# In a slot, the weight copy ahead of plan pieces and results, and plan pieces at other steps

## The reference, cut to what matters

```python
# x [32, 128, 128], ctx [32, 128, 256], mask [32, 128]; 8 heads of 16; 8 experts of 512; fp32
h = layernorm(x)
kv = (ctx @ W_src.T + b_src) * mask;  q = (h @ W_tgt.T + b_tgt) * mask
attn = softmax(where(mask == 0, -inf, q @ k.T / 4));  upd = attn @ v
x = x + tanh(g_xattn) * (concat([h, upd]) @ W_out.T + b_out)
t = layernorm(x)
p = softmax(t @ router_w.T);  top 2 of 8, weights renormalised
x = x + tanh(g_ffn) * sum over the 2 experts e of weight * (gelu(t @ w1[e]) @ w2[e])
```

## Time and profile before

| | us |
|---|---|
| median of 3 runs (lowest, highest) | 334.58 (333.62, 334.91) |
| the profiled execution, its span | 335.18, 333.4 |
| PE busy | 301.5 (90%) |
| weight loads (PEld) | 267.2 (80%) |
| DVE busy | 213.8 (64%) |
| POOL busy | 202.9 (61%) |
| ACT busy | 189.2 (57%) |
| mean granted TensorE clock | 0.974 |

### The profile page before, as it was taken

How to read it: one execution, slowest core, us unless ns; L and a number is a source line. 1 busy time by engine, 2 the same in 40 slices (tenths; PEclk the granted TensorE clock), 3 DMA queues, 4 the chain that set the end, 5 groups by cost and what they waited for, 6 DMA issues and landing times.

```text
span 333.4 us, 11014 instructions
## 1 busy us (share of the span) xinstructions
PE 301.5 (90%) x3649; PEld 267.2 (80%) x3649; DVE 213.8 (64%) x909; ACT 189.2 (57%) x470; POOL 202.9 (61%) x269
## 2 busy tenths in 40 slices
PE   8699899999999999997988979999998999999920
PEld 3577787787878878785778969999998999999910
DVE  3647566679888887889567896336852334335653
ACT  3276758778696886867585427547444444444400
POOL 3523334233686868857455878878878875656850
PEclk9999999999999999999799997999999999999985
DMA  6524612202131211850144122311353442139346
GB/s 217 176 90 160 219 39 66 60 24 96 49 111 53 66 50 49 248 145 31 53 100 113 58 68 79 89 50 50 96 124 95 130 114 78 60 124 307 96 131 189
DMA packets 41237, 34.61 MB, mean 104 GB/s; under 512 B 5044, under 2 KB 36950, under 8 KB 41184
## 3 DMA queue, kind: packets, MB, share of 16 engines
q1 hardware_dynamic: 32608, 23.10, 24.1%
q0 software_dynamic: 4320, 8.47, 7.1%
q10 hardware_dynamic: 4256, 2.36, 2.4%
HBM read 22.35 MB, written 12.01 MB: 103 GB/s over the span
## 4 chain that ended last, share of the span: by engine, by line
PE 46%; POOL 22%; issue 14%; DVE 9%; ACT 4%; DMA 3%; POOLq 0%; SPq 0%; ACTq 0%; DVEq 0%
POOL rows L639 10%; PE ps_sc L1573 9%; POOL picked L657 8%; PE ps_o L1532 4%; PE ps_proj L1586 4%; PE ps_o L1586 4%; PE ps_sc L1416 3%; PE ps_proj L1461 3%; PE ps_sc L1426 3%; PE ps_proj L1464 3%; PE ps_sc L1411 2%; DVE rowmax L1205 2%; ACT xr L781 2%; POOL pscratch L652 2%; PE ps_xT L1455 1%
## 5 line engine op out<-in xcount | busy, mean ns | idle before, releaser
L657 POOL DMA_INDIRECT picked<-yo,xg x71 | 71.5, 1008 | 16.2 <-issue 11.3
L1573 PE MATMUL ps_sc<-xt,w1c 128*128 128x128 f32 x568 | 76.1, 277 | 3.0 <-issue 2.4
L639 POOL DMA_INDIRECT rows<-xr,posi x64 | 63.3, 989 | 18.0 <-issue 18.0
L1573 PEld LDWEIGHTS ps_sc<-xt,w1c 128*128 128x128 f32 x568 | 69.8, 194 | 3.9 <-issue 3.9
L815 ACT ACTIVATE probT<-ps_sc 128x512 f32<-128x512 f32 x71 | 42.5, 598 | 43.0 <-PE ps_sc L1573 43.0
L1205 DVE TENSOR_REDUCE rowmax<-ps_sc 128x4 f32<-128x512 f32 x64 | 43.7, 691 | 26.5 <-PE ps_sc L1430 22.3
L710 ACT ACTIVATE probT<-ps_sc,pencol 128x512 f32<-128x512 f32 x64 | 43.6, 683 | 21.3 <-PE ps_sc L1430 19.1
L587 POOL TENSOR_TENSOR kblk<-kT,headcol 128x256 f32<-128x256 f32 x32 | 19.7, 617 | 51.7 <-ACT kT L739 51.5
L1586 PE MATMUL ps_proj<-w2s,probT 128*128 x288 | 38.9, 279 | 0.0
L1586 PE MATMUL ps_o<-w2s,probT 128*128 x280 | 37.1, 275 | 0.0
L1323 DVE COPY w1c<-w1s 128x512 f32 x71 | 31.6, 448 | 7.1 <-PE ps_sc L1573 2.3
(11 more groups left out here) (166 smaller groups left out, 589.9 us busy)
## 6 DMA issues: line engine op xcount, KB each, us to landing
xg<-rows SPq DMA_DIRECT2D x71, 65.0 KB, 1.8
ctxs<-ctxT SPq DMA_DIRECT2D x32, 128.0 KB, 2.1
xs<-x SPq DMA_DIRECT2D x8, 256.0 KB, 3.1
maskbc<-mask SPq DMA_DIRECT2D x8, 256.0 KB, 3.8
w1s<-w SPq DMA_DIRECT2D x4, 512.0 KB, 3.6
w2s<-w SPq DMA_DIRECT2D x8, 256.0 KB
maskbc<-picked SPq DMA_DIRECT2D x4, 512.0 KB, 6.6
out<-xs ACTq DMA_DIRECT2D x6, 256.0 KB, 2.3
```

What stands on the lines that cost most here:

```text
L639: nc.gpsimd.indirect_dma_start(out=rows, out_offset=bass.IndirectOffsetOnAxis(ap=posi[:, i, pick, b:b + 1], axis=0), in_=xr[:, i, pick, b, ...
L657: nc.gpsimd.indirect_dma_start(out=picked, out_offset=bass.IndirectOffsetOnAxis(ap=xg[:, r, D + 1:D + 2].bitcast(I32), axis=0), in_=yo[:, ...
L1573: last = nc.tensor.matmul(ps_score[j % DEEP][:, c * 128:(c + 1) * 128], w1c[:, j % DEEP, c * 128:(c + 1) * 128], xt[:, j % XRING, :], star ...
```

## The change

In DVE's `slot`, the copy of the weights moves from behind ranks and plan pieces to the front; the result stays last. The middle plan's `carry` is cut in two: its two sums become a piece of their own (`sum_open`), so that the middle plan has eight pieces, in slots 6 to 13 (before: seven, in slots 6 to 12). Of the first plan's pieces, 0 stays at (8, 0), 1 at (8, 1); 2 and 3 come to (8, 1) too (before: (8, 2) and (8, 3)), and 4 to (8, 3) (before: (9, 0)).

```diff
+                def sum_open():
+                    sums(last, stop, 2, late_exp, late_row)
+
                 def carry():
                     count = stop - last
-                    sums(last, stop, 2, late_exp, late_row)
                     then(nc.vector.tensor_tensor(lead[:, :], bounds[:, EXPERTS:EXPERTS + 1],
...
-                return count_full, end_full, pass_ends, write, end_open, pass_open, carry
+                return count_full, end_full, pass_ends, write, end_open, pass_open, sum_open, carry
...
-                piece = {(8, 0): 0, (8, 1): 1, (8, 2): 2, (8, 3): 3, (9, 0): 4}.get((g, k))
-                if piece is not None:
+                for piece in {(8, 0): (0,), (8, 1): (1, 2, 3), (8, 3): (4,)}.get((g, k), ()):
                     first_pieces[piece]()
...
             def slot(n):
+                j = slot_of(n, 0)
+                if j is not None:
+                    if j % REGS == 0:
+                        turn["experts"] = experts_of(mybir.EngineType.DVE, j, min(REGS, SLOTS - j))
+                    wait(dve, f_up, j - DEEP + 1)
+                    nc.vector.tensor_copy(
+                        w1c[:, j % DEEP, :],
+                        w1s[:, turn["experts"][j % REGS], :].rearrange("p o h -> p (o h)")).then_inc(f_w1, 1)
                 for G in range(GROUPS):
                     if in_slots(G) and n == ranked_at(G) + 1:
...
                 if n in late_pieces:
                     late_pieces[n]()
-                j = slot_of(n, 0)
-                if j is not None:
-                    if j % REGS == 0:
-                        turn["experts"] = experts_of(mybir.EngineType.DVE, j, min(REGS, SLOTS - j))
-                    wait(dve, f_up, j - DEEP + 1)
-                    nc.vector.tensor_copy(
-                        w1c[:, j % DEEP, :],
-                        w1s[:, turn["experts"][j % REGS], :].rearrange("p o h -> p (o h)")).then_inc(f_w1, 1)
                 j = slot_of(n, LAG_DOWN)
```

## The result

| | before | after |
|---|---|---|
| median of 12 runs each, us (lowest, highest) | 334.6 (332.93, 335.54) | 336.94 (334.93, 339.03) |
| ratio, 95% interval | | 1.0077 [1.0057, 1.0097] |
| profiled execution, span, us | 335.18, 333.4 | 338.35, 336.5 |
| mean granted TensorE clock of it | 0.974 | 0.966 |

The time lies just outside the range, on the slow side, and the forecast (335.0, no change) was wrong. The runs of the changed kernel spread over 4 us, and the slow ones have the lower clock: 334.93 us at 0.980, 336.25 at 0.973, 338.12 at 0.967, 339.03 at 0.965; the profiled one, 338.35 at 0.966, is the second slowest of the twelve.

A forecast was written before the change was run, and what follows sets the result against it. The prediction took POOL's sends and scatters, then PE from slot 41 on, as the bound; 335.18 + 0 (slot order) + 0.4 (pieces) = 335.6 us profiled, 335.0 on the median's footing, range 332.9 to 336.9.

The forecast's parts named there:

- The slot's order, what it moves: Slot 12's copy goes ahead of the carry: up-projection 2.2 us sooner, 0.75 us wait for slot 8's result, 3.2 us won.
- It can't keep them: PE's 3.2 us are gone by 207.81, as ACT's normalisation in step (10, 3) waits for POOL's mr2; term 0.
- these two places: POOL's mr2, awaited by ACT, and slot 41's load behind POOL's last scatter: each would take PE's 3.2 us.
- The half clock behind the new wait: Rival at 205.8: PE falls to half clock (1.7 us), 1.7 - 0.87 uncovered at slot 41; +0.8, 335.8 us, chance 0.04.
- POOL's stretch has a fixed length: From slot 1's result to group 7's last scatter POOL waits for nobody, about 73 us; slot 41 follows its end.
- the prediction's own test: Wrong if POOL's stretch is under 72 us or broken by DVE waits, or slot 41 moves over 1.7 us from 255.93.
- The first plan's pieces: DVE's rowmax of (9, 0) comes 0.4 us later, and POOL's start and slot 41 with it; +0.4, bounds 0 and +1.6.
- Slower, by (8, 2): Rival: PE idles in (8, 2) for a rowmax 1.6 us late and its clock falls; +2.1, 336.7 us, chance 0.10.
- The clock stays up at (9, 0): Rival: moved pieces split PE's 1.48 us wait at (9, 0), keeping up to 1.7 us; 333.3 us, chance 0.10.
- POOL held up by moved copies: Rival: eight moved DVE copies block POOL's descriptor writing, 8 x 0.43 = 3.4 us; 338.4 us, chance 0.02.

The follow-up runs named there:

- e6: The changed kernel with POOL's rs2 and mr2 of group 7 computed earlier, in slot 9 ahead of its sends: 337.33 us, ratio 1.008.
- e7: Kernel before plus new slot order and cut carry, POOL's group 7 rs2 and mr2 in slot 9, its eight scatters in slot 29; old pieces: 330.28 us, 0.9856.
- e2: Kernel before with only the slot's new order and the cut carry, first plan's pieces as before: 335.22 us, ratio 1.0024.
- e5: The changed kernel run again, unaltered, in another measurement: 337.19 us, ratio 1.0061.
- e10: Kernel before with only the slot's new order and the cut carry, measured a second time on another chip: 335.88 us, ratio 1.0048.
- e4: Kernel before with eleven matmuls of unused result filling PE's 2.4 us wait ahead of slot 12's up-projection: 334.47 us, ratio 1.0003.
- e1: Kernel before with only the first plan's pieces moved, slot order and carry as before: 334.54 us, ratio 1.0008.
- e3: The changed kernel with thirteen matmuls of unused result filling PE's wait for xt in slot 16: 335.04 us, ratio 1.0009.
- e8: Kernel before with only the POOL edits: group 7's rs2 and mr2 in slot 9, its eight scatters in slot 29: 333.43 us, ratio 0.9959.
- e9: The whole change plus both POOL edits: group 7's rs2 and mr2 in slot 9, its eight scatters in slot 29: 331.52 us, ratio 0.9898.

## Why the prediction was wrong

**The slot's order, what it moves: right.** The copy of slot 12 runs at 196.15, the up-projection starts 2.4 us sooner (forecast 2.2), the down-projection of slot 10 waits 0.47 us for slot 8's result (forecast 0.75), and the clock is whole at 201. DVE by time, after, answers to the earlier trace rows:

```profile
196.15 0.43 DVE L1311 COPY w1c<-w1s 128x512 f32 x1 [0.28 <-PE ps_sc L1574]
196.49 0.65 DVE L1096 TENSOR_REDUCE late_exp<-skipped 128x30 f32<-128x480 f32 x1
197.18 0.65 DVE L1097 TENSOR_REDUCE late_row<-gone 128x30 f32<-128x480 f32 x1
197.86 0.35 DVE L1332 TENSOR_SCALAR yo<-ps_proj,xg 128x128 f32<-128x128 f32 x1
```

**It can't keep them: right.** ACT idles 4.37 us for `mr2` and the times behind it hang on POOL. ACT by time, after, answers to the earlier trace rows:

```profile
204.53 1.65 ACT L781 ACTIVATE xr<-xs,mr,rs 128x128 f32<-128x128 f32 x4 [4.37 <-POOL mr L607]
206.08 0.25 ACT L806 ACTIVATE xt<-ps_sc 128x128 f32<-128x128 f32 x1
206.35 1.28 ACT L815 ACT_TABLE_LOAD   x1
207.65 0.60 ACT L815 ACTIVATE probT<-ps_sc 128x512 f32<-128x512 f32 x1
```

That even a gain that passed would end at slot 41 is what e6 shows, and e7 shows that it was these two places and no third.

**The half clock behind the new wait: the step that failed.** The prediction named it, took 0 for it, put its bound at +0.8 (1.7 us less a cover of 0.87 us at slot 41), and gave it a chance of 0.04. Three things were wrong. It was the likely case: all four profiles with the new order and the wait left open show it (after, e2, e5, e10), and the 2.4 us wait of the earlier trace rows, behind which the clock had fallen, was reason to expect the same of a 3 us wait. Its cover was looked for in the wrong place: the first to feel a late PE is POOL, whose send needs slot 13's result, with 0.11 us to spare; slot 41's 0.87 us cover PE, not POOL, and e2 and e10 are late at slot 41 while PE still idles there. And its size is not that of one stretch: 0.7 to 0.9 us in three profiles, but about 2.8 us in the profile of the result. That the first lies near the bound's +0.8 is luck: the bound was reckoned from PE's cover at slot 41, while in e2 and e10 it was POOL's wait for slot 13's result (1.15 and 0.85 us) that for the most part came through. For the same reason "POOL's stretch has a fixed length" did not hold: the earlier trace rows showed that POOL waited for nobody, not by how much; the prediction's own test (broken by waits for DVE, or slot 41 over 1.7 us late) found both.

Put otherwise, the change moved a half clock from ahead of a wait for ACT, where e4 shows that it cost nothing, to behind it, where it delays a result that POOL wants.

**The first plan's pieces: right in kind, 0.70 us instead of 0.4.** DVE by time, after, answers to the earlier trace rows:

```profile
145.12 0.35 DVE L1267 SCALAR_TENSOR_TENSOR qT<-ps_proj,wts,maskbc 128x128 f32<-128x128 f32 x1 [1.00 <-ACT vals L742]
...
156.75 0.17 DVE L1102 SCALAR_TENSOR_TENSOR slot_row<-sgone,iota 128x25 int32<-128x25 f32 x1
156.96 0.18 DVE L1104 TENSOR_SCALAR slot_exp<-sexp 128x25 int32<-128x25 f32 x1
157.18 1.48 DVE L1207 TENSOR_REDUCE rowmax<-ps_sc 128x4 f32<-128x512 f32 x2
```

From the end of DVE's idling to that rowmax it is 12.06 us against 11.56 in the earlier trace rows: +0.50, the forecast's own reading. The other 0.2 us is the rowmax itself, whose two operations take 1.48 us and not 1.29; why was not tried. PE's turn in (9, 0) then comes at 158.76 behind 1.32 us, at 158.35 behind 1.48.

**The rivals.** *Slower, by (8, 2)*: PE idles there, but for 0.57 us and with no drop of the clock, so it does not decide. *The clock stays up at (9, 0)*: the profile after has it at 0.50 at 161 to 162, as the earlier trace rows; it falls in some executions and not in others, with the old pieces and with the new (see the last section). *POOL held up by moved copies*: its sends took 1021 ns and its scatters 983, a difference of 38 ns where the earlier trace rows had 42; the copies' new place did nothing to it. From 178 us to the last scatter, the sends and scatters that lay over a weight copy (29 before, 27 after) took 1.00 and 1.01 us on average, the others 0.99 in both. The Trainium skill's rule (SBUF — State Buffer, "SBUF: two separate sides"), by which GpSimd can't write DMA descriptors while such a copy runs, does not show in these durations.

**The sum with the measured terms**: 334.58 + 0.70 + 0.8 = 336.1 us, inside the range; the measured median is 336.94, and the ratio makes it 334.58 x 1.0077 = 337.2. Times at a like clock bear the two terms out. Over all executions with a mean granted clock of 0.977 or more, the medians are 333.80 us for the kernel before (29 of 72 executions beside e1 to e10), 334.42 with the pieces alone (8 of 12), 334.47 with the order alone (10 of 24) and 335.26 with both (5 of 21): +0.6, +0.7 and +1.5 us. The remaining 0.8 to 1.1 us of the median come from executions at a lower clock: it is 0.968 or less in 7 of the 21 of the changed kernel (337.3 us and more), but in 2 of the 72, none of the 12 and 2 of the 24. They can be executions like the profiled one, in which the half clock lasts longer. That is not shown, for a run without a profile shows only its time and mean clock, and whether it takes the pieces and the order together to bring them about was not tried. By their ratios e1, e2 and e10 (0.08%, 0.24% and 0.48%) come to less than the 0.6 to 0.8% of the whole, within their intervals.

## What to carry to other kernels

Where an edit moves a wait and doesn't end it, ask where the clock of TensorE will be low afterwards and who wants the next result: here a half clock ahead of a wait was free, and the same behind it was not. "Waits for nobody" is no measure of room: for each engine on the path, subtract the time at which its input is ready from the time at which it uses it (here 0.11 us). A local gain is had only once each later bound is moved with it: the same slot order was +0.2 to +0.5% alone and worth 3.15 us, for 330.28 us in all, after two edits to POOL's order.

## What the runs showed of the hardware

Behind like waits the clock stayed at 0.50 for different times: to about 208, 209 and 212 us in e10, e2 and e5 (some 3.4 us each), and for 6.8 us in the profile of the result and in e6. It need not fall only once PE works again: in e6 it fell 3.0 us into a wait of 4.81 us, and in e10 some 0.2 us before the wait for xt ended. Behind the wait of 1.3 to 1.5 us at (9, 0) it fell in six of the twelve profiles (before, after, e5, e7, e8, e9) and not in the other six, whatever the pieces: from PE's turn of that rowmax to POOL's release it was 19.8 to 20.1 us with the fall and 18.4 to 18.5 without, so 1.5 us come and go between executions of one kernel. Matmuls whose results nobody reads, put into a wait, kept the clock at 1.00 (e3, e4). The last scatter took 2.3 to 2.4 us to land in seven of the ten profiles whose chain holds it, but 2.72 in e9, 3.33 in e7 and 3.38 in that of the result; what lengthened it was not tried.
